# Token scatters of six tiles held back behind VectorE's products of the shared units

## The chip, the cores and the metric

One core of a Trainium2 chip runs the whole kernel. The metric is device time in microseconds of an execution; lower is better. Before the change it is 340.23 us, the median of three runs (339.7 to 340.44).

## The reference

One transformer block with adaptive layer norm on 2 x 1024 tokens of width 256. Attention comes first (causal, one head), then a feed-forward part with a shared expert and 16 routed experts, of which each token uses four.

```python
h = layernorm(x) * (1 + ca) + sa
x = x + ga * attention(h)
h = layernorm(x) * (1 + cb) + sb
probs = softmax(h @ w_router); top_w, top_i = top_k(probs, 4); top_w /= sum(top_w)
routed = sum over the four experts e of top_w[e] * (silu(h @ we1[e]) * (h @ we3[e])) @ we2[e]
shared = (silu(h @ ws1) * (h @ ws3)) @ ws2
x = x + gb * (shared / 5 + routed * 4 / 5)
```

## The kernel before

**Tiles and stages.** The 2048 tokens are 16 tiles of 128, `t` = 0 to 15; tile t is the (t+1)-th, so the eleventh is t = 10. A loop over steps s runs attention with a tile in each of several stages, and sends normed rows to the router. Four tiles make a group. For each group VectorE picks four experts a token (`route_choose`, `route_count`), TensorE counts ranks (`rank`), and VectorE turns them into slots, places in a DRAM tensor `xg_rows` sorted by expert (`route_slots`, which ends in the write of `slot_u`, line 1347, and adds one to `s_slots`).

**Scatters.** GpSimd's `send` writes the rows of a tile to their slots: four indirect DMAs a tile, one for each choice k, 128 rows of 1152 bytes each (line 776). The first 32 are sent inside the loop over steps (`SENDS`). The last 32, tiles t = 8 to 15, go in one call behind the loop. Ahead of a tile's first scatter GpSimd waits for the tile's row and for the slots of its group. Every scatter adds 16 to `s_sent`. Behind the scatters GpSimd's queue holds only the scatters of the routed results (line 817).

**The shared expert.** It is cut into 16 units, `n` = 0 to 15, four (quarters of the hidden width) for each block of 512 tokens. For each unit TensorE computes both products (`gate_up`, lines 1816 to 1818), ScalarE applies silu (`silu_step`, line 911), VectorE multiplies (`g_step`, line 1461; it adds one to `s_g`), and TensorE applies the down product (`down`, line 1990). Units 0 to 11 stand ahead of the routed experts, 12 to 15 behind them. In VectorE's queue the products of units 4 to 11 have between them: the tables of the routed tiles (`route_places`, `route_tables`, `route_marks`), the sums of finished blocks (`shared_out`), and the low parts of the routed weights (`split_routed`, lines 1450 to 1454, 16 subtractions of 128x768, from a table `splits` by n).

**The routed experts.** The sorted rows are cut into 40 pairs of tiles of 128 rows. SyncE loads them from `xg_rows` (`load_rows`, line 645), two loads of 144 KB a pair, into a ring of four pairs. It begins when all 64 scatters have landed. From the fifth pair on a load waits for VectorE's `s_rxlo` of four pairs before. VectorE first copies two words a row (`keep_ends`, line 1744), TensorE transposes the rows (`rows_back`, line 2191), ScalarE and VectorE split them in two parts, TensorE multiplies with the expert's weights, ScalarE applies silu (line 1083), and so on up to GpSimd's scatter of the results.

**The places where it meets.** SyncE's queue around the first load:

```python
if n == 0:
    sp.wait_ge(s_sent, 16 * TILES * TOPK)
if n >= RING:
    sp.wait_ge(s_rxlo, n - RING + 1)
load_rows(n, place[2 * (n % 8):2 * (n % 8) + 2], s_xs[n % RING])
```

TensorE's queue goes `down(11)` for the first two token tiles, `rows_back(0)`, `down(11)` for the other two, `rows_back(1)`, and then the pairs. VectorE's goes `g_step(11)`, `split_routed(15)`, `x_lo_rows(0)` (which begins with `keep_ends(0)`), `shared_out(2)`, and then the pairs.

Of the kernel before, what the change touches and what calls it, by code (L numbers as in the profile page):

```python
# [190 lines left out]
ROUTER_CONSTANTS = 10 + len(TOKEN_RUNS)  # L191


SENDS = {9: 4, 10: 4, 11: 4, 12: 4, 13: 4, 14: 4, 15: 4, 16: 4}


# [39 lines left out]
def adaln_block(nc, x, qkv, o_proj, gamma, beta, w_router, we1, we3, we2, ws1, ws3, ws2, c_in, wmod, out):  # L236
# [3 lines left out]
    with ctx:  # L240
        def sem(name):
            return ctx.enter_context(nc.semaphore(name))
# [253 lines left out]
        def done(eng, stage_, t):  # L496

            if t >= 0:
                eng.wait_ge(tl[stage_], t + 1)
# [11 lines left out]
        s_ab, s_y, s_silu, s_g, s_gated, s_shared = (sem(n) for n in (  # L511
            "gate_up_mm", "down_mm", "silu", "g", "shared_gated", "shared_added"))
# [175 lines left out]
        def _(pool):  # L688
# [33 lines left out]
            def token_numbers():  # L722

                for t, token, count in TOKEN_RUNS:
                    nc.gpsimd.iota(tok_at[:, t:t + count], pattern=[[1, count]], base=token, channel_multiplier=BT,
                                   allow_small_or_imprecise_dtypes=True).then_inc(s_ones2, 1)
# [39 lines left out]
            def send(count):  # L766


                for n in range(sent[0], sent[0] + count):
                    t, k = divmod(n, TOPK)  # L770
                    if n == 0:
                        pool.wait_ge(s_regions, 16 * 5)
                    if k == 0:
                        done(pool, "h2row", t)
                        pool.wait_ge(s_slots, t // BT + 1)
                    nc.gpsimd.indirect_dma_start(  # L776
                        out=xg, out_offset=bass.IndirectOffsetOnAxis(ap=slot_u[:, t, k:k + 1].bitcast(U32), axis=0),
                        in_=hrow[:, t, :], in_offset=None).then_inc(s_sent, 16)
                sent[0] += count

            for s in range(FIRST, LAST + 2):
                if -3 < s < 0:
                    residual(s + 3)
                for m, group in enumerate(norms_of(s)):
                    if s == -3 and m == 1:
                        residual(0)
                    inverse_std(group)
                    for n, t in reversed(group):
                        if n > 1:
                            mean_shift(n, t)  # L790
                if 0 <= s and s + 3 < RESIDUAL_BY_VECTOR:

                    done(pool, "rinv", s - 1)
                    residual(s + 3)
                if s == 3:
                    router_constants()
                if s == 5:
                    token_numbers()
                send(SENDS.get(s, 0))

# [4 lines left out]
            for r in range(RING):  # L805
                nc.gpsimd.memset(sent_all[:, :, r:r + 1], 16.0 * loads_of(NPAIR - RING + r)).then_inc(s_mark_const, 1)
            send(TILES * TOPK - sent[0])


# [1484 lines left out]
```

## Time and profile before

| what | value |
|---|---|
| time, median of 3 runs | 340.23 us (339.7 to 340.44) |
| the profiled execution | span 380.7 us; the page gives no other time for it |
| TensorE busy | 333.3 us (88% of the span), mean granted clock 0.990 |
| VectorE busy | 255.2 us (67%) |
| ScalarE busy | 190.3 us (50%) |
| GpSimd busy | 200.8 us (53%), of it 65.6 in 64 scatters of line 776 and 70.5 in 72 of line 817 |
| DMA | 57.55 MB, mean 151 GB/s |

The span runs from the first to the last instruction of the one execution that the hardware profiler recorded. It is longer than the timed runs, which are taken without the profiler. A share of 0.50 in the granted clock is 1.2 GHz, 1.00 is 2.4 GHz.

### The profile page before, as it was taken

What the parts mean: (1) busy time and instruction counts of PE and PEld (TensorE: products, weight loads), DVE (VectorE), ACT (ScalarE), POOL (GpSimd) and SP (SyncE); (2) the same over time, 40 slices, a digit from 0 to 9 for tenths busy, and PEclk for the clock granted to TensorE, in tenths of its full rate; (3) what the DMA queues carried; (4) which work ended last, traced back from release to release, by engine and by line L of the source; (5) the groups of instructions that cost most, each with busy time, mean ns of one, the idle gap of its engine ahead of it and who ended that gap; (6) DMA issues with size and microseconds to landing.
All of it is one profiled execution on the core that took longest, in us unless ns stands there. A gap on an engine that the chain in (4) does not pass through costs nothing.

```text
span 380.7 us, 7758 instructions
## 1 busy us (share of the span) xinstructions
PE 333.3 (88%) x2252; PEld 297.6 (78%) x2252; DVE 255.2 (67%) x806; ACT 190.3 (50%) x440; POOL 200.8 (53%) x285
## 2 busy tenths in 40 slices
PE   8989999999999999868889897788778877887995
PEld 5778898888899898736778796777667767877784
DVE  1889998999887756219986744543454345448797
ACT  2667777767865665414234444443444355346300
POOL 2687754357867655746740064555455545545820
PEclk9999999999999999969999999999999999999999
DMA  8236600002213996322232466556445544788824
GB/s 271 75 104 205 209 17 27 16 31 87 85 65 118 316 312 214 119 85 78 104 117 76 121 209 183 155 171 194 149 124 171 164 133 136 264 302 327 261 86 165
DMA packets 42280, 57.55 MB, mean 151 GB/s; under 512 B 5144, under 2 KB 34592, under 8 KB 42240
## 3 DMA queue, kind: packets, MB, share of 16 engines
q1 hardware_dynamic: 34288, 35.42, 30.7%
q0 software_dynamic: 6864, 19.80, 13.5%
q10 hardware_dynamic: 1088, 1.84, 1.5%
q8 instruction: 20, 0.33, 0.4%
q14 instruction: 20, 0.16, 0.2%
HBM read 32.64 MB, written 24.40 MB: 150 GB/s over the span
## 4 chain that ended last, share of the span: by engine, by line
PE 43%; DVE 27%; issue 13%; another core or an unknown queue 7%; ACT 7%; DMA 1%; POOL 1%; DVEq 0%; ACTq 0%
PE ps L1816 10%; PE ps L1818 10%; PE ps L1817 9%; PE ps L1990 4%; DVE y_in L1497 3%; DVE r_g L1771 2%; DVE gT_lo L1759 2%; ACT r_silu L1083 2%; DVE negmax L1626 2%; PE ps L2191 2%; PE ps L2092 1%; PE ps L1823 1%; DMA wmod_sb<-in_L_wmod_dram 1%; DVE bn L1197 1%
## 5 line engine op out<-in xcount | busy, mean ns | idle before, releaser
L817 POOL DMA_INDIRECT y_rows<-y_sb,aside x72 | 70.5, 980 | 87.9 <-ACT y_sb L1092 71.7
L776 POOL DMA_INDIRECT xg_rows<-hrow,slot_u x64 | 65.6, 1024 | 27.8 <-issue 20.0
L1816 PE MATMUL ps<-rpool 128*128 128x256 f32 (+3 forms) x152 | 49.8, 328 | 2.7 <-DVE rpool L1221 1.1
L1768 DVE TENSOR_TENSOR aside<-ends,aside 128x2 int32<-128x2 int32 (+1 forms) x40 | 6.3, 157 | 62.9 <-ACT r_silu L1083 55.4
L1816 PE MATMUL ps<-w_hi_routed,xT_hi 128*128 x158 | 45.2, 286 | 1.8 <-DVE xT_lo L1752 1.8
L1083 ACT ACTIVATE r_silu<-ps 128x256 f32<-128x256 f32 x40 | 15.8, 395 | 61.4 <-PE ps L1818 51.4
L1818 PE MATMUL ps<-rpool 128*128 128x256 f32 (+3 forms) x152 | 46.0, 302 | 0.0
L1817 PE MATMUL ps<-rpool 128*128 128x256 f32 (+3 forms) x152 | 45.9, 302 | 0.0
L1818 PE MATMUL ps<-w_hi_routed,xT_lo 128*128 x158 | 44.7, 283 | 0.0
L1817 PE MATMUL ps<-w_lo_routed,xT_hi 128*128 x158 | 44.6, 283 | 0.0
L1816 PE MATMUL ps<-w_hi_routed,gT_hi 128*128 x79 | 25.8, 326 | 15.1 <-DVE gT_lo L1759 15.0
L1816 PEld LDWEIGHTS ps<-rpool 128*128 128x128 f32 x152 | 28.8, 190 | 6.0 <-DVE rpool L1221 2.5
L1816 PEld LDWEIGHTS ps<-w_hi_routed,xT_hi 128*128 128x128 f32 x158 | 30.2, 191 | 2.5 <-issue 2.3
L1752 DVE TENSOR_TENSOR xT_lo<-ps,xT_hi 128x512 fp32r<-128x512 f32 x40 | 27.4, 684 | 6.2 <-ACT xT_hi L1071 6.0
L1817 PEld LDWEIGHTS ps<-w_lo_routed,xT_hi 128*128 128x128 f32 x158 | 30.2, 191 | 0.0
L1818 PEld LDWEIGHTS ps<-w_hi_routed,xT_lo 128*128 128x128 f32 x158 | 30.2, 191 | 0.0
L1816 PEld LDWEIGHTS ps<-w_hi_routed,gT_hi 128*128 128x128 f32 x79 | 14.9, 188 | 19.5 <-issue 19.4
L1818 PEld LDWEIGHTS ps<-rpool 128*128 128x128 f32 x152 | 28.8, 189 | 1.1
L1817 PEld LDWEIGHTS ps<-rpool 128*128 128x128 f32 x152 | 28.9, 190 | 0.9
L1816 PE MATMUL ps<-h2T_hi,w_hi_shared 128*128 128x512 f32 x64 | 27.3, 426 | 1.4 <-issue 0.9
L1071 ACT ACTIVATE xT_hi<-ps 128x512 fp32r<-128x512 f32 x40 | 24.4, 612 | 8.0 <-remote 5.8
L1817 PE MATMUL ps<-h2T_lo,w_hi_shared 128*128 128x512 f32 x64 | 25.6, 400 | 2.6 <-issue 2.6
(236 smaller groups left out, 928.8 us busy)
## 6 DMA issues: line engine op xcount, KB each, us to landing
xs<-xg_rows SPq DMA_DIRECT2D x68, 144.0 KB
y_in<-y_rows SPq DMA_DIRECT2D x16, 512.0 KB
xg_rows<-empty SPq DMA_DIRECT2D x4, 576.0 KB, 3.8
x_in<-in_L_attn_x_dram SPq DMA_DIRECT2D x16, 128.0 KB, 2.1
w_raw_routed<-in_L_ffn_we_dram SPq DMA_DIRECT2D x8, 256.0 KB
out_dram<-x SPq DMA_DIRECT2D x14, 128.0 KB, 1.8
xs_own<-xg_rows SPq DMA_DIRECT2D x11, 144.0 KB
wmod_sb<-in_L_wmod_dram ACTq DMA_DIRECT2D x3, 512.0 KB, 6.6
```

The source lines that it names most:

```text
L776: nc.gpsimd.indirect_dma_start(out=xg, out_offset=bass.IndirectOffsetOnAxis(ap=slot_u[:, t, k:k + 1].bitcast(U32), axis=0), in_=hrow[:, t, ...
L817: nc.gpsimd.indirect_dma_start(out=yb, out_offset=bass.IndirectOffsetOnAxis(ap=dest[:, 2 * n + i:2 * n + i + 1].bitcast(U32), axis=0), in_ ...
L1071: nc.scalar.activation(xT_hi[:, n % 2].rearrange("p i c t -> p (i c t)"), ps[:, 6 + n % 2, :], ACT.Copy).then_inc(s_rxhi, 1)
L1083: nc.scalar.activation(r_silu[:, n % 2], ps[:, n % 2, :].rearrange("p (i w) -> p i w", i=2)[:, :, 0:H], ACT.Silu).then_inc(s_rsilu, 1)
L1497: then(nc.vector.tensor_tensor(y[0], y[0], y[k], ALU.add))
L1626: nc.vector.tensor_reduce(negmax[:, t % 4:t % 4 + 1], score_banks(t), AX.X, ALU.max, negate=True).then_inc(tl["negmax"], 1)
L1752: nc.vector.tensor_tensor(xT_lo[:, n % 2].rearrange("p i c t -> p (i c t)"), ps[:, 6 + n % 2, :], xT_hi[:, n % 2].rearrange("p i c t -> p ...
L1759: nc.vector.tensor_tensor(gT_lo[:, n % 2].rearrange("p i t -> p (i t)"), ps[:, 2 + n % 2, 0:2 * P], gT_hi[:, n % 2].rearrange("p i t -> p ...
L1816: nc.tensor.matmul(dst, w[0], x_[0], start=first, stop=False)
L1817: nc.tensor.matmul(dst, w[0], x_[1], start=False, stop=False)
L1818: return nc.tensor.matmul(dst, w[1], x_[0], start=False, stop=last)
L1990: last = nc.tensor.matmul(to, unit(n)[1][:, tok], w_raw_s[:, e, W2:WX], start=(e == 0 and b < NB - 1 and j % 2 == 0), stop=(e == SH - 1), ...
```

## The change

GpSimd's `send` gets one more wait ahead of the first scatter of tiles t = 10 to 15. Tile 10 waits until `s_g` has reached 5, that is until `g_step(4)`, the fifth product, is done; tile 11 for the sixth, and so on up to tile 15 for the tenth. Tiles 8 and 9 are not held. No instruction is moved on any engine's queue; only these six waits are added.

```diff
+SENT_BEHIND = {10: 4, 11: 5, 12: 6, 13: 7, 14: 8, 15: 9}
 SENDS = {9: 4, 10: 4, 11: 4, 12: 4, 13: 4, 14: 4, 15: 4, 16: 4}
...
                     if k == 0:
                         done(pool, "h2row", t)
                         pool.wait_ge(s_slots, t // BT + 1)
+                        if t in SENT_BEHIND:
+                            pool.wait_ge(s_g, SENT_BEHIND[t] + 1)
                     nc.gpsimd.indirect_dma_start(
```

## Rows read from the trace of the kernel before

**Rows 1.** The page: its head, and the chain by engine.
```profile
span 380.7 us, 7758 instructions
...
PE 43%; DVE 27%; issue 13%; another core or an unknown queue 7%; ACT 7%; DMA 1%; POOL 1%; DVEq 0%; ACTq 0%
```

**Rows 2.** SyncE's queue: its waits (us, times, longest), and its timeline (start, us).
```profile
SPq L644 <- DMA xg_rows<-hrow,slot_u: 9.8, 1, 9.8
...
196.94 0.90 SPq L645 DMA_DIRECT2D xs<-xg_rows  x2
```

**Rows 3.** Timelines of TensorE and VectorE at the first routed rows: start, us, what.
```profile
203.17 4.49 PE L1990 MATMUL ps<-w_raw_shared,act_g 128*128 128x256 f32 x20
207.50 0.60 PE L2191 MATMUL ps<-ident,xs 128*128 128x128 f32 x4
...
208.80 0.60 PE L2191 MATMUL ps<-ident,xs 128*128 128x128 f32 x4
...
207.39 0.23 DVE L1744 TENSOR_SCALAR ends<-xs 128x2 int32 x2
```

**Rows 4.** DMA issues (KB each, us to landing); a window: busy, clock, DMA share, GB/s.
```profile
xg_rows<-empty SPq DMA_DIRECT2D x1, 144.0 KB, 2.1
...
204.50:206.90 2.40, 2.40 (x13) 2.02 (x12) 1.14 (x3) 1.33 (x2) 0.00 (x0) 1.00 0.00 0
```

**Rows 5.** Timeline of GpSimd from the ninth tile's scatters on.
```profile
147.30 1.08 POOL L776 DMA_INDIRECT xg_rows<-hrow,slot_u  x1 [1.12 <-DVE slot_u L1347]
...
166.43 0.96 POOL L776 DMA_INDIRECT xg_rows<-hrow,slot_u  x1 [0.30 <-issue]
173.05 0.96 POOL L776 DMA_INDIRECT xg_rows<-hrow,slot_u  x1 [5.66 <-DVE slot_u L1347]
...
189.85 1.63 POOL L776 DMA_INDIRECT xg_rows<-hrow,slot_u  x1 [0.30 <-issue]
...
194.32 0.96 POOL L776 DMA_INDIRECT xg_rows<-hrow,slot_u  x1 [0.30 <-issue]
219.43 0.96 POOL L817 DMA_INDIRECT y_rows<-y_sb,aside  x1 [24.16 <-ACT y_sb L1092]
```

**Rows 6.** Timeline of VectorE: the last slots, and products 5, 6, 7, 8, 10.
```profile
171.84 0.42 DVE L1347 TENSOR_REDUCE slot_u<-matched 128x16 int32<-128x256 f32 x1
...
172.51 0.68 DVE L1461 SCALAR_TENSOR_TENSOR act_g<-act_g,ps 128x512 f32<-128x512 f32 x1
...
175.72 0.68 DVE L1461 SCALAR_TENSOR_TENSOR act_g<-act_g,ps 128x512 f32<-128x512 f32 x1
...
184.37 0.68 DVE L1461 SCALAR_TENSOR_TENSOR act_g<-act_g,ps 128x512 f32<-128x512 f32 x1
...
188.23 0.68 DVE L1461 SCALAR_TENSOR_TENSOR act_g<-act_g,ps 128x512 f32<-128x512 f32 x1
...
197.20 0.68 DVE L1461 SCALAR_TENSOR_TENSOR act_g<-act_g,ps 128x512 f32<-128x512 f32 x1
```

**Rows 7.** Around 158 to 170: chain; VectorE; windows (PE, PEld, DVE, ACT, POOL, clock, DMA).
```profile
158.68 11.34 another core or an unknown queue
...
170.05 0.22 DVE L1315 TENSOR_TENSOR above<-ps,region 128x64 f32<-128x64 f32 x1 [11.37 <-remote]
...
159.00:162.00 3.00, 1.54 (x6) 0.96 (x6) 0.00 (x0) 1.57 (x3) 2.39 (x3) 1.00 0.41 153
...
165.00:168.00 3.00, 1.85 (x3) 0.68 (x3) 0.00 (x0) 0.00 (x0) 1.93 (x2) 0.50 0.28 108
```

**Rows 8.** Timeline of ScalarE in the routed stage: silu of pairs.
```profile
220.00 0.39 ACT L1083 ACTIVATE r_silu<-ps 128x256 f32<-128x256 f32 x1 [0.84 <-PE ps L1818]
...
222.81 0.39 ACT L1083 ACTIVATE r_silu<-ps 128x256 f32<-128x256 f32 x1
...
236.52 0.38 ACT L1083 ACTIVATE r_silu<-ps 128x256 f32<-128x256 f32 x1 [3.69 <-PE ps L1818]
...
244.14 0.38 ACT L1083 ACTIVATE r_silu<-ps 128x256 f32<-128x256 f32 x1 [3.66 <-remote]
```

## The prediction, made before the changed kernel had run

> **What bounds the kernel now.** I read the page first. The profiled execution spans 380.7 us [rows 1], and the median of the three timed runs is 340.23 us, so 40.5 us of the profile are not in the timed runs. The page gives no other time for that execution. A term read from it may be carried over only if it is a difference between two paths of the same stage, and I choose such differences below. The chain of waits is TensorE's for 43% and VectorE's for 27%. The chain names no scatter and no load of routed rows, so the scatters are off the critical path today.
>
> Second, I asked when the routed rows must be there. SyncE waits 9.8 us for the last scatter (its row names that as the releaser) and issues its first load of sorted rows at 196.94 [rows 2]. TensorE works without a pause through the shared units until 207.50, when it transposes the first routed rows. VectorE reads them first at 207.39 [rows 3].
>
> How long do the rows take from there? The first two loads belong to pair 0, and their two issues take 0.90 us [rows 2]. A load of the same 144 KB with no neighbour took 2.1 us to land [rows 4]. So pair 0 lands 2.1 to 3.0 us after SyncE's start; I estimate 2.7, that is 199.6, for the second issue begins within those 0.90. The far bound is the end of all eight first loads: nothing moves after 204.5 [rows 4]. So today pair 0 waits in SBUF for about 207.4 - 199.6 = 7.8 us. That slack is what the change spends.
>
> Third, GpSimd. Tiles 9 to 12 (eleventh tile is t = 10, so these are t = 8 to 11) go out in one train from 147.30 to 166.43, a scatter each 1.27 us. Then it waits for the slots of the last group, ready at 172.26, and t = 12 to 15 go from 173.05 to 194.32 [rows 5]: 15 steps in 21.27 us. SyncE starts 196.94 - 194.32 = 2.6 us after the last one begins.
>
> **The change, part by part.** It adds six waits on GpSimd's queue, moves no instruction and removes nothing. The product that t waits for is the 5th to the 10th: the 5th starts at 172.51, the 6th at 175.72, the 7th at 184.37, the 8th at 188.23 and the 10th at 197.20, each takes 0.68 [rows 6].
>
> t = 10 and 11. Today they are the second half of the train that ends at 166.43, in an interval in which GpSimd is otherwise free until 173.05. With the change they leave after 173.2 and 176.4: eight scatters more stand ahead of t = 12. A scatter starts 0.8 us after what released it (slots end 172.26, scatter 173.05 [rows 5, 6]), so t = 10 starts at 174.0, t = 11 at 174.0 + 4 x 1.27 = 179.1, done by 184.2.
>
> t = 12. It waits for the seventh product, which ends at 184.37 + 0.68 = 185.05, so it starts at 185.85. Today it is 173.05. The shift is 12.8 us.
>
> t = 13, 14, 15. A tile takes 21.27 / 15 x 4 = 5.7 us, so they are reached at 191.5, 197.2 and 202.9. The products end at 188.9, before 197.2 (the 9th lies ahead of the 10th) and at 197.9: these three waits are met on arrival and cost nothing. What covers them is GpSimd's own pace; were a scatter free, t = 15 would go at 198.7.
>
> The end of the train is 185.85 + 21.27 = 207.1. SyncE starts 2.6 us later, 209.7, and pair 0 is in at 209.7 + 2.7 = 212.4. TensorE and VectorE want it at 207.4. **The new wait is 5.0 us.** Bounds: with no scatter lengthened the train is 15 x 1.27 = 19.05 us and the wait 2.8; if pair 0 took as long as all eight loads do today (204.5), 4.9 us more, but that is four pairs, and the lone load is nearer, so I keep 2.7. What makes the train 2.2 us longer than its shortest are a few scatters of up to 1.63 instead of 0.96 [rows 5] that lie beside VectorE's subtractions of routed weights (lines 1450 to 1454). Ten such subtractions lay in that train, and eleven follow the seventh product, so I keep 21.27.
>
> The Trainium skill has a rule here that speaks against the change ("SBUF — State Buffer", section "Who interferes with whom"): a VectorE instruction with two SBUF inputs and a GpSimd instruction that reads SBUF exclude each other for the whole instruction. By it each of eleven subtractions could hold the train for its full length, some 10 us in all instead of the 2.2 that the train shows over its shortest. The trace agrees with the direction and not with that size.
>
> Does this difference hold in the timed runs? The seventh product to the first routed transposition is 207.50 - 185.05 = 22.4 us of nearly unbroken TensorE work, and the seventh product to landed rows is 0.8 + 21.3 + 2.6 + 2.7 = 27.4. Both start from the same event, so whatever the profile adds before 185 cancels. This is why I measure from the product and not from the clock of the trace.
>
> Who is behind the waits? On GpSimd only the later scatters, then the scatters of results, first at 219.43 [rows 5]; they wait for ScalarE's rows and move with them. SyncE's queue holds the loads. VectorE stands at its first copy from the rows, with its last shared sum behind it, and TensorE at its transposition, with half a unit of the shared down product behind it. So nobody fills the gap. Pair 1 is issued right behind pair 0 and TensorE wants it 1.3 us later (207.50 to 208.80 [rows 3]); what little it may add stays in the range. From there each stage waits for the one before it, and the whole rest moves by 5.0.
>
> **TensorE's clock.** In the span it falls once before the end. It was 1.00, then TensorE was busy 1.54 of 3 us from 159 on, and from 165 to 168 it was 0.50 of 2.4 GHz, that is 1.2 GHz [rows 7]. A gap of 5.0 us is idler than that, so it may fall again. At the lower level the first transpositions and the half unit, 208.80 - 207.50 = 1.3 us of work ahead of everything, take twice as long: +1.3, or 0. I take half, 0.7.
>
> Sum: 340.2 + 5.0 + 0.7 = 345.9.
>
> **The rivals.** *Faster: the burst was the trouble.* From 158.68 the chain holds 11.34 us that the profile puts down to nothing on this core, VectorE waits 11.37 for TensorE's ranks, and TensorE is busy for half of the time from 159 to 162 [rows 7]. This is just when t = 10 and 11 go out, and it ends when their packets are out. If the scatters cause it and the timed runs have it too, the change gives back up to 11.35 and pays 5.0: 340.2 - 6.3 = 333.9. It decides from 5.0 us of stall on. Against it: GpSimd scatters as densely from 173.05 to 194.32 [rows 5] without such a gap, and the DMA share was only 0.41 and 0.28 in the stall [rows 7]. And the routed stage has waits of the same kind, ScalarE idle 3.66 us in every second pair [rows 8]: two pairs take 244.14 - 236.52 = 7.62 us there, where two of the first pairs took 2 x (222.81 - 220.00) = 5.62. Of 40 pairs some 33 go at the slow pace: 16.5 x 2.0 = 33 us, and with the stall 44, near the 40.5 that the timed runs lack. So I read both as the cost of being profiled. The skill has a path for this ("NOTIFIC — the notification-queue block", section "Overflow: three behaviours, one of which stalls the engine"): the records' internal pipeline holds up an engine rather than lose one. No row here shows that pipeline. Chance 0.13.
>
> *No change: the slack is larger in the timed runs.* Without the stall TensorE reaches the routed rows 11.35 earlier and t = 12 goes right behind t = 11, at 167.7 instead of 173.05, 5.35 earlier; slack 7.8 - 11.35 + 5.35 = 1.8, shift 185.85 - 11.35 - 167.7 = 6.8, and again 5.0. Only a shorter train (2.8 at the least by the rows) and a slower TensorE together bring it under 0.7. 340.2. Chance 0.09.
>
> *Slower still:* the timed runs have no slack at all and the clock falls: 6.8 + 1.3 = 8.1, 348.3. It needs TensorE to be 1.8 us faster to the routed rows than in the profile. Chance 0.08.
>
> **How the numbers follow.** The forecast, a starved start of the routed stage, has 0.70; its own range is 2.8 to 5.0 + 1.3 + 1.5 for a longer train, 343.0 to 348.0. Faster has 0.13, no change 0.09, slower still 0.08. "No change" means within 0.2%, 0.7 us, about what a measurement of this kernel can tell. Slower by more is 0.70 + 0.08 = 0.78. The range must leave out at most 2 in 10: it takes in the forecast's own, no change, and nearly all of slower still, 339.8 to 348.4; the faster case stays out.
>
> **What would show it.** In the new profile t = 12 starts 0.8 us after the seventh product, and t = 13 to 15 go without a pause. The last scatter starts some 22 us after the seventh product. SyncE's first load of sorted rows is issued about 2.6 us after that. The first routed transposition has an idle time of 4 to 6 us ahead of it with a load of rows as releaser, and the granted clock shows whether 0.50 comes behind it. The forecast is wrong if TensorE goes from the shared units to the routed rows without a pause. The rival is right if the time falls and nothing like the 11.34 us stands between the rank product and the slots; should only the profiled span get shorter, that stall was the profile's own.

## The result, and the profile after

The changed kernel takes 348.0 us (median of 4 runs, 346.69 to 349.17), the kernel before, on the same chip, 340.34 us (4 runs, 339.7 to 340.47). The ratio is 1.0232, with a 95% interval of 1.021 to 1.0254: 7.7 us slower. The forecast was 345.9, with the range 339.8 to 348.4.

First the page of the changed kernel: head, busy times, clock, and the chain by engine. Its execution took 346.69 us, with a span of 345.0, so unlike that of [rows 1] it is of a piece with the timed runs.

```profile
span 345.0 us, 7758 instructions
...
PE 324.1 (94%) x2252; PEld 297.8 (86%) x2252; DVE 256.0 (74%) x806; ACT 195.9 (57%) x440; POOL 202.3 (59%) x285
...
PEclk9999999999999999999999969999999999999999
...
PE 54%; DVE 21%; issue 10%; POOL 7%; ACT 4%; DMA 2%; DVEq 0%; SPq 0%; ACTq 0%; POOLq 0%
```

GpSimd and the DMA now stand in the chain of what ended last, with 7% and 2%, where they had 1% each [rows 1], and 2% and 1% in the second profile of the kernel before that is shown below. One slice of the clock reads 6, just past the middle. The waits of the same kernel (total us, times, longest):

```profile
SPq L645 <- DMA xg_rows<-hrow,slot_u: 23.3, 1, 23.3
...
POOL xg_rows L779 <- DVE act_g L1464: 7.7, 2, 5.3
...
DVE ends L1747 <- DMA xs<-xg_rows: 6.6, 1, 6.6
PE ps L2194 <- DMA xs<-xg_rows: 6.3, 1, 6.3
```

Two things are new. GpSimd stood twice for a product of VectorE, and TensorE and VectorE each stood once for routed rows that had not landed. The timelines say where. VectorE's seventh product, then GpSimd: the last scatter that goes unheld, the first of t = 10, the first of t = 12, one of the long ones, and the last of all.

```profile
173.46 0.68 DVE L1464 SCALAR_TENSOR_TENSOR act_g<-act_g,ps 128x512 f32<-128x512 f32 x1
...
155.56 0.96 POOL L779 DMA_INDIRECT xg_rows<-hrow,slot_u  x1 [0.30 <-issue]
161.81 0.95 POOL L779 DMA_INDIRECT xg_rows<-hrow,slot_u  x1 [5.28 <-DVE act_g L1464]
...
174.94 0.96 POOL L779 DMA_INDIRECT xg_rows<-hrow,slot_u  x1 [2.38 <-DVE act_g L1464]
...
178.95 1.63 POOL L779 DMA_INDIRECT xg_rows<-hrow,slot_u  x1 [0.30 <-issue]
...
196.63 0.96 POOL L779 DMA_INDIRECT xg_rows<-hrow,slot_u  x1 [0.30 <-issue]
```

SyncE's first load, and TensorE at the seam between the shared and the routed expert:

```profile
199.27 10.77 SPq L646 DMA_DIRECT2D xs<-xg_rows  x12
...
191.19 4.49 PE L1993 MATMUL ps<-w_raw_shared,act_g 128*128 128x256 f32 x20
202.01 1.11 PE L2194 MATMUL ps<-ident,xs 128*128 128x128 f32 x4 [6.33 <-DMA xs<-xg_rows]
...
209.14 0.38 PE L1819 MATMUL ps<-w_hi_routed,xT_hi 128*128 x1 [1.57 <-DVE xT_lo L1755]
```

And windows over the seam (stretch and length, busy time of PE, PEld, DVE, ACT and POOL, granted clock, DMA share, GB/s):

```profile
195.70:198.70 3.00, 0.00 (x0) 0.00 (x0) 0.00 (x0) 0.00 (x0) 1.59 (x2) 1.00 0.29 112
198.90:202.00 3.10, 0.00 (x0) 0.00 (x0) 0.00 (x0) 0.00 (x0) 0.00 (x0) 0.50 0.48 130
202.00:205.50 3.50, 3.49 (x13) 3.03 (x14) 1.64 (x5) 0.60 (x1) 0.00 (x0) 0.50 0.77 224
206.00:209.00 3.00, 1.57 (x14) 1.33 (x12) 2.79 (x10) 1.36 (x3) 0.00 (x0) 1.00 0.25 77
```

Read them together. The seventh product ends at 174.14, and 0.80 later t = 12 starts. The last scatter starts 21.69 us after that, SyncE's first load 2.64 after it, and TensorE has its rows 2.74 after that, at 202.01. TensorE had been done with its shared work since 195.68, and did nothing for 6.33 us. During that pause its clock went to 0.50 (1.2 GHz), and the four transpositions take 1.11 instead of 0.60 us [rows 3]. From the first transposition to the first product of pair 1 it is 209.14 - 202.01 = 7.13 us.

### The profile page after: what moved, and what is told of

Same layout as the page of the kernel before. It is cut to its first block, busy times and chain, and to the rows that moved or that the text cites. A ratio compares the mean times of both kernels' runs of the same rounds, so it can differ in the third digit from the quotient of the medians.

```text
span 345.0 us, 7758 instructions
## 1 busy us (share of the span) xinstructions
PE 324.1 (94%) x2252; PEld 297.8 (86%) x2252; DVE 256.0 (74%) x806; ACT 195.9 (57%) x440; POOL 202.3 (59%) x285
## 4 chain that ended last, share of the span: by engine, by line
PE 54%; DVE 21%; issue 10%; POOL 7%; ACT 4%; DMA 2%; DVEq 0%; SPq 0%; ACTq 0%; POOLq 0%
PE ps L1819 13%; PE ps L1820 12%; PE ps L1821 12%; PE ps L2194 5%; POOL xg_rows L779 5%; DVE y_in L1500 3%; PE ps L1993 3%; PE ps L2220 2%; DVE negmax L1629 2%; PE ps L2095 1%; PE ps L1826 1%; DMA wmod_sb<-in_L_wmod_dram 1%; PE ps L1928 1%; DVE bn L1200 1%; DVE y_in L1510 1%
## 5 line engine op out<-in xcount | busy, mean ns | idle before, releaser
L779 POOL DMA_INDIRECT xg_rows<-hrow,slot_u x64 | 66.6, 1040 | 29.5 <-issue 19.4
L2194 PE MATMUL ps<-ident,xs 128*128 128x128 f32 x136 | 21.3, 281 | 6.3 <-DMA xs<-xg_rows 6.3
L1821 PE MATMUL ps<-h2T_hi,w_lo_shared 128*128 128x512 f32 x64 | 25.1, 392 | 0.0
```

The source lines that it names most:

```text
L779: nc.gpsimd.indirect_dma_start(out=xg, out_offset=bass.IndirectOffsetOnAxis(ap=slot_u[:, t, k:k + 1].bitcast(U32), axis=0), in_=hrow[:, t, ...
L1821: return nc.tensor.matmul(dst, w[1], x_[0], start=False, stop=last)
L2194: last = nc.tensor.transpose(ps[:, 6 + n % 2, (i * DC + c) * P:(i * DC + c + 1) * P], rows_of(n)[i][:, c * P:(c + 1) * P], ident[:])
```

## The experiments

### The kernel before once more

The 380.7 us of [rows 1] fit no timed run. I needed a profile of the kernel before that does. The edit is none.

> The kernel before, unchanged, once more for a second profile. If the 11.34 us stall and the slow pace of the routed pairs (7.62 us for two) were only in that one recorded execution, this profile spans about 338.5 us, as the changed kernel's spans 345.0 at a time of 346.69: no wait of VectorE over 5 us between the rank product and the slots, and pairs 2.81 us apart. TensorE then reaches the first routed transposition at about 195.5 with the load of rows landed 1 to 2 us before. If scatters in a burst stall TensorE in the timed runs too, the stall of about 11 us is there again and the span stays near 338 only because something else is shorter. Time: 340.3, ratio 1.000.

Measured: 339.91 us against 339.95, ratio 0.9997 (0.9972 to 1.0021). The profiled execution took 340.43 us, its span is 338.7. Its windows at the place of [rows 7] (columns as above), its last scatter and first load, and TensorE at the seam:

```profile
span 338.7 us, 7758 instructions
...
159.00:162.00 3.00, 3.00 (x15) 2.54 (x14) 2.86 (x13) 1.22 (x2) 2.19 (x3) 1.00 0.26 100
165.00:168.00 3.00, 3.00 (x15) 2.48 (x14) 2.06 (x4) 2.07 (x3) 2.39 (x3) 1.00 0.34 134
...
190.56 0.96 POOL L776 DMA_INDIRECT xg_rows<-hrow,slot_u  x1 [0.30 <-issue]
...
193.41 9.96 SPq L645 DMA_DIRECT2D xs<-xg_rows  x12
...
196.60 0.60 PE L2191 MATMUL ps<-ident,xs 128*128 128x128 f32 x4
...
202.48 0.38 PE L1816 MATMUL ps<-w_hi_routed,xT_hi 128*128 x1 [1.66 <-DVE xT_lo L1752]
```

TensorE is busy 3.00 of 3 us where it had 1.54 and 1.85, at full clock, and the 11.34 us of stall are not there, although t = 10 and 11 go out at the very same place. So the scatters do not cause it, and the rival "the burst was the trouble" has nothing to give back. The pairs of the routed stage follow 2.81 us apart nearly throughout, so the slow pace of [rows 8] was of that one recorded execution too. What caused it there is not shown.

The same profile gives the true slack. With 2.74 us from first load to use, pair 0 would be usable at 193.41 + 2.74 = 196.15, and TensorE wants it at 196.60. The slack is about 0.45 us, not the 7.8 of the recorded execution. And 202.48 - 196.60 = 5.88 us there become 7.13 after the change: with nearly the same second gap (1.66 and 1.57), the low clock costs 1.25 us. So 6.33 + 1.25 = 7.6 of the measured 7.7 us. The whole way from the end of the seventh product to that first product of pair 1 gives the same: 202.48 - 175.24 = 27.24 us before, 209.14 - 174.14 = 35.00 after, 7.76 more. The spans of the two profiled executions differ by less, 6.3 us, mainly because the one of the changed kernel ended its seventh product 1.10 us earlier; it is also the fastest of its four.

### One tile's wait at a time

The edit is the table alone. For t = 12:

```diff
-SENT_BEHIND = {10: 4, 11: 5, 12: 6, 13: 7, 14: 8, 15: 9}
+SENT_BEHIND = {12: 6}
```

> Only the thirteenth tile (t = 12) waits, for the seventh product. My theory: this one wait sets the start of the last four tiles, so all of the loss is here: last scatter some 21.7 us after t = 12's first, t = 12 at 174.9, gap of TensorE 6.3 us, time 348, +7.7 within 0.7. Rival (each of the six waits, or the spreading of scatters over a longer stretch, costs a part): clearly less, +2 to +5.

Then `{10: 4, 11: 5}` alone:

> Only t = 10 and 11 wait, for the fifth and sixth product. My theory: t = 10 starts at 161.8 as in the changed kernel, t = 11 at 167.3, and t = 12 follows without a pause at about 172.9, 2.1 us earlier than with all six waits: gap of TensorE 6.3 - 2.1 = 4.2 us; time +4.2 if the granted clock stays at 1.00, +5.4 if it falls to 0.50 behind the gap. Rival (the seventh product's wait is all that counts): 0.

Then `{13: 7}`, `{14: 8}` and `{15: 9}`, each alone:

> Only the wait of t = 13 (for the 8th product) is left. Theory: the 8th product ends at 179.10, t = 13 starts at 179.9 instead of about 174.0, the shift is 5.9, less 0.8: gap 5.1 us, and the clock falls as in e3, 1.2 more: 340.0 + 6.3 = 346.3. If the clock stays, 345.1. Rival (only t = 12's wait can cost, the later ones nothing): 340.0.

> Only the wait of t = 14 (for the 9th product) is left. Theory: the 9th product ends at 182.31 in e1's profile, t = 14 starts 0.8 later at 183.1 instead of about 180.0, the shift is 3.1, less 0.8 of slack: gap 2.3 us, clock as before, 342.3. Rival (costs nothing alone either): 340.0.

> Only the wait of t = 15 (for the 10th product) is left. Theory (the slack behind the last scatter is only about 0.8 us in timed executions, as the profiled run of e1 shows against after's; so every hold counts by how far it moves the last scatter, less 0.8): in e1's profile the 10th product ends at 186.97 and t = 15 is reached at about 185.0 + 0.8, so its first scatter moves by about 2.0 us, TensorE's gap ahead of the first routed rows is about 1.2 us, the clock stays at 1.00, and the time is 340.0 + 1.2 = 341.2. Rival (the prediction's 'the waits of t = 13 to 15 are met on arrival and cost nothing'): no change, 340.0, no gap.

TensorE's row at the first routed transposition in each of the five, in the order t = 12; 10 and 11; 13; 14; 15:

```profile
202.54 1.12 PE L2194 MATMUL ps<-ident,xs 128*128 128x128 f32 x4 [6.52 <-DMA xs<-xg_rows]
...
201.86 1.12 PE L2194 MATMUL ps<-ident,xs 128*128 128x128 f32 x4 [5.06 <-DMA xs<-xg_rows]
...
201.12 1.11 PE L2194 MATMUL ps<-ident,xs 128*128 128x128 f32 x4 [5.06 <-DMA xs<-xg_rows]
...
199.09 0.65 PE L2194 MATMUL ps<-ident,xs 128*128 128x128 f32 x4 [2.39 <-DMA xs<-xg_rows]
...
195.96 0.66 PE L2194 MATMUL ps<-ident,xs 128*128 128x128 f32 x4 [0.55 <-DMA xs<-xg_rows]
```

Set beside the end of VectorE's seventh product, an event that all of them share, they fall in line. "First load" is SyncE's first load less the end of that product; the shift is this less the 18.17 of the kernel before (193.41 - 175.24). "Seam" is the time from the first routed transposition to the first product of pair 1, 5.88 us in the kernel before.

| holds | first load | shift | TensorE's gap | shift less gap | lowest clock | seam | time, against before |
|---|---|---|---|---|---|---|---|
| all six | 199.27 - 174.14 = 25.13 | 6.96 | 6.33 | 0.63 | 0.50 | 7.13 | 348.0, 340.34 |
| t = 12 | 199.61 - 174.48 = 25.13 | 6.96 | 6.52 | 0.44 | 0.50 | 7.15 | 347.78, 339.95 |
| t = 10, 11 | 199.13 - 175.25 = 23.88 | 5.71 | 5.06 | 0.65 | 0.50 | 8.14 | 346.91, 339.95 |
| t = 13 | 198.37 - 174.54 = 23.83 | 5.66 | 5.06 | 0.60 | 0.50 | 8.16 | 346.16, 340.07 |
| t = 14 | 196.34 - 175.22 = 21.12 | 2.95 | 2.39 | 0.56 | 1.00 | 5.94 | 343.23, 340.07 |
| t = 15 | 193.13 - 173.90 = 19.23 | 1.06 | 0.55 | 0.51 | 1.00 | 5.94 | 340.57, 340.07 |

Every hold opens a gap as long as the shift of the first load, less 0.4 to 0.7 us of slack, and where the clock falls its share comes on top. Which tile is held matters through where the last scatter ends. The ratios of the rows from t = 12 to t = 14 are 1.0243 (1.0205 to 1.0281), 1.0202 (1.0157 to 1.0247), 1.0177 (1.0155 to 1.0199) and 1.01 (1.0073 to 1.0126). For t = 15 it is 1.0 (0.9981 to 1.002): a gap of 0.55 us is too small to be timed, so the row shows it and the runs neither confirm nor refute it.

The clock's share was not the same in all. In the two profiles with a gap of 5.06 us the seam takes 8.14 and 8.16 us, 2.3 more than before the change and not the 1.25 of the changed kernel. The row that ends it for t = 10 and 11:

```profile
210.00 0.38 PE L1819 MATMUL ps<-w_hi_routed,xT_hi 128*128 x1 [1.57 <-DVE xT_lo L1755]
```

The clock fell there only 1.0 and 0.9 us before TensorE began again, in the changed kernel 3.2 before, and the low stretch was 6.8 us long in each. So more work fell on it, and the shorter gap saved only part of its 1.3 us. Both are the slowest of their four executions (348.07 and 347.19 us), so 2.3 need not hold for the other three.

Two expectations of gaps were missed. For t = 10 and 11 it was 4.2 us and came out as 5.06: t = 12 did go 2.0 us earlier than with all six holds, but its train took 22.25 us instead of 21.69, and the load came 2.82 after its last scatter instead of 2.64. With the larger share of the clock the time was +7.0, where +4.2 or +5.4 was expected. For t = 15 the gap was to be 1.2 and was 0.55: t = 15 was held for 2.0 us as expected, but its four scatters, of which fewer now ran beside long instructions of VectorE, took 4.06 us from first to last instead of 4.79.

The holds do not add: together they cost what the one costs that delays the train most, since a scatter held early waits in time that would be waited later anyway. t = 12 alone is as slow as all six. The waits of t = 13 to 15 are free only while t = 12's stands ahead: alone, t = 13's costs 6.1 us and t = 14's 3.2, near the 6.3 and 2.3 that were expected.

The holds of t = 10 and 11 cost nearly as much, which the recorded execution could not show. There GpSimd was idle for 5.66 us, until 173.05 [rows 5], waiting for slots that the stall had delayed. In the undisturbed execution the slots of the last group end at 161.17, well ahead, and GpSimd has no idle time from t = 8 to t = 15. Its train is one piece, so a pause anywhere in it moves the end, by about its length.

### The gap filled

The changed kernel, with 26 more products on TensorE ahead of the first routed transposition. Nobody reads what they write.

```diff
+            for _ in range(26):
+                nc.tensor.matmul(ps[:, 0, :], w_hi_s[:, 0, 0:P], h2T_hi[:, 0, 0, :], start=True, stop=True)
             rows_back(0)
```

> The changed kernel with 26 extra products of 128x512 on TensorE ahead of the first routed transposition, 26 x 0.228 = 5.9 us, written to a bank that the next product overwrites. My theory: the wait for the rows stays at 6.3 us, of which TensorE now works 5.9, so the clock stays at 1.00 and only the clock's share of the loss goes: from 202.0 to the second pair's first product 5.9 us instead of 7.1, time 346.7, that is +6.4. Rival (the clock costs nothing, the whole loss is the wait): +7.7 as with the change alone.

Measured: 346.33 us, ratio 1.0184 (1.0143 to 1.0226). That is 6.4 us over the kernel before beside it, as expected, where the changed kernel was 7.7 over its own. The two intervals overlap, so the time alone does not settle it; the trace does. TensorE's rows:

```profile
196.28 6.27 PE L2239 MATMUL ps<-h2T_hi,w_hi_shared 128*128 128x512 f32 x26
202.92 0.66 PE L2194 MATMUL ps<-ident,xs 128*128 128x128 f32 x4 [0.37 <-DMA xs<-xg_rows]
...
208.85 0.38 PE L1819 MATMUL ps<-w_hi_routed,xT_hi 128*128 x1 [1.65 <-DVE xT_lo L1755]
```

The clock stayed at 1.00 and 208.85 - 202.92 = 5.93 us, against 7.13 with the gap open and 5.88 in the kernel before. So the pause lowers the clock, and that costs 1.2 us here; the rest is the late rows and stays. In the table above the clock fell for gaps of 5.06 us and more and not for 2.39. What lies between was not tried.

### Real work in the gap

The changed kernel, with what stood behind the late rows moved ahead of them.

```diff
+            shared_out(UNITS_FIRST // SH - 1)
             x_lo_rows(0)
-            shared_out(UNITS_FIRST // SH - 1)
...
-            down(UNITS_FIRST - 1, range(0, BT // 2))
+            down(UNITS_FIRST - 1)
             rows_back(0)
-            down(UNITS_FIRST - 1, range(BT // 2, BT))
             rows_back(1)
```

> The changed kernel with the work that stood behind the late rows moved ahead of them: on TensorE all of the shared down product of unit 11 before the first routed transposition, on VectorE the third shared sum (2.5 us) before the first copy from the rows. Theory (the loss is a starved start; what TensorE and VectorE can do meanwhile comes back): TensorE's gap shrinks by the 0.8 us of the last matmuls at full clock, the second gap of 1.6 us (behind VectorE's sum) goes, so 348.0 - 2.4 = 345.6; the gap of about 5.5 us still lowers the clock to 0.50, which is why it isn't better. Rival (the time is set by the landing of the rows and the pace of pairs alone, and the second gap stands whatever is ahead, since ScalarE holds the second pair's rows back behind its silu): 348.0 - 0.8 = 347.2.

Measured: 347.96 us, ratio 1.0223 (1.0195 to 1.025), no gain over the changed kernel. My theory of 345.6 is refuted. TensorE, and ScalarE at its side:

```profile
202.47 1.11 PE L2194 MATMUL ps<-ident,xs 128*128 128x128 f32 x4 [5.46 <-DMA xs<-xg_rows]
203.96 1.11 PE L2194 MATMUL ps<-ident,xs 128*128 128x128 f32 x4 [0.38 <-DMA xs<-xg_rows]
...
210.01 0.58 PE L1819 MATMUL ps<-w_hi_routed,xT_hi 128*128 x1 [1.16 <-DVE xT_lo L1755]
...
208.04 0.39 ACT L1086 ACTIVATE r_silu<-ps 128x256 f32<-128x256 f32 x1 [3.83 <-PE ps L1821]
208.32 1.17 ACT L1074 ACTIVATE xT_hi<-ps 128x512 fp32r<-128x512 f32 x2
```

The first gap shrank by 0.9 us as it should. The second gap shrank only from 1.57 to 1.16 us, since VectorE's sum was not its only cause: ScalarE copies the rows of pair 1 (208.32) only behind the silu of pair 0 (208.04). The part of the rival that names ScalarE holds, and its 347.2 lies within the interval. In this profiled execution (349.49 us) the clock also stayed at 0.50 for twice as long, 13.7 us, until 213.03, which slows the products ahead of that silu too. The mean clock was 0.978 there and 0.989, 0.988 and 0.985 in the other three, against the changed kernel's 0.99 and once 0.987; how often the long stretch comes is not shown. The other three alone, 346.99 to 348.23 us, are above 345.6 as well.

### Versions that could beat both

That second gap of 1.66 us is in the kernel before too. The edit to the kernel before takes the copy of pair 1 ahead on ScalarE and its low part on VectorE:

```diff
             x_hi(0)
+            x_hi(1)
...
-                if n == 0:
-                    x_hi(1)
...
             x_lo_rows(0)
+            x_lo_rows(1)
             shared_out(UNITS_FIRST // SH - 1)
...
-                if n == 0:
-                    x_lo_rows(1)
```

> The kernel before, with the high and low parts of the second routed pair taken ahead: ScalarE's copy of pair 1 right behind that of pair 0 (was behind the silu of pair 0), and VectorE's low part of pair 1 right behind that of pair 0, ahead of the third shared sum. In e1's profile TensorE stands 1.66 us at 202.48 for this low part. Theory (rows landed early leave a start of the stage that only the order of ScalarE's and VectorE's queues holds back): that gap goes, 340.0 - 1.6 = 338.4. Rival (the sum of 2.5 us now stands ahead of the products of pair 0, and the gap only moves to the third pair): 340.0, within 0.5.

Measured: 339.3 us against 339.92, ratio 0.9991 (0.9975 to 1.0007): not told apart from the kernel before, and not the 1.6 us of the theory. Run again beside the next version:

> The kernel of e8 again, beside e10 on the same chip. Theory: 0.6 us under the kernel before (e8: 339.3 against 339.9) and 0.7 over e10. Rival (e8's 0.6 was chance): as the kernel before.

Measured: 339.32 us against 340.09, ratio 0.9969 (0.9952 to 0.9986). That is a small gain, 0.8 us in the medians. The gap of 1.66 us is gone, but 0.26 and 0.39 us came back at pair 2, where TensorE now waits for VectorE, which does its 2.5 us sum just before. Theory and rival of the first run each had a part:

```profile
203.34 0.44 PE L2215 MATMUL ps<-ident,r_g 128*128 128x128 f32 x2 [0.26 <-DVE r_g L1770]
204.16 0.38 PE L1814 MATMUL ps<-w_hi_routed,xT_hi 128*128 x1 [0.39 <-DVE xT_lo L1751]
```

The last version is that kernel once more changed. It moves the addition of that sum behind the low part of pair 2 and leaves only its two products in front:

```diff
                 if n + 2 < NPAIR:
                     x_lo_rows(n + 2)
+                if n == 0:
+                    shared_add(UNITS_FIRST // SH - 1)
```

> e8 with the third shared sum cut in two: VectorE's two products (1.28 us) stand behind the low part of pair 1, its addition (1.22 us) behind the low part of pair 2. In e8's profile the products of pair 0 start 1.25 us after the end of the shared products, and TensorE then stands 0.25 and 0.39 us for VectorE at the third pair. Theory (the start of the routed stage is VectorE's queue; the 1.66 us gap of the kernel before comes back in full once the whole sum no longer stands there): no gap over 0.3 us, 340.0 - 1.4 = 338.6. Rival (e8 had all there was, since later pairs wait for something else): as e8, 339.3.

Measured: 338.54 us against 340.09 (12 and 23 runs), ratio 0.9963 (0.9945 to 0.9981). Of the waits at the start of the routed stage 0.20 and 0.31 us are left (the first, ahead of pair 0's first product, is in the kernel before too):

```profile
196.81 0.38 PE L1821 MATMUL ps<-w_hi_routed,xT_hi 128*128 x1 [0.20 <-DVE xT_lo L1756]
...
203.43 0.38 PE L1821 MATMUL ps<-w_hi_routed,gT_hi 128*128 x1 [0.31 <-DVE gT_lo L1763]
```

It is faster than both kernels, than the one before by 1.3 us by the ratio and 1.55 in the medians, as expected; that is well under 2%. That it also beats the version with the sum in one piece (0.8 us in the medians) is likely, but the two intervals overlap.

## Why the prediction was right, and where its sizes were off

**What bounds the kernel.** "The scatters are off the critical path today" was right, but barely. The slack of 7.8 us was read from an execution with a stall in front of the seam, and the estimate of 1.8 for the timed runs was still too high: about 0.5. The shift that went with it, 6.8, was nearly right: 6.96.

**t = 12, the step that carries the sum.** Right. t = 12 started 0.80 us after the seventh product, as taken, and no later tile waited. Measuring from that product, and not from a point of the trace's clock, is what saved the sum from the 40 us of disturbance. The wait was 6.3 and not 5.0, and both paths of the difference had their part: scatters to landed rows 27.9 us (0.80 + 21.69 + 2.64 + 2.74) where the text had 27.4, and TensorE 195.68 - 174.14 = 21.5 where it had 22.4. The mis-sized term is the second above all: the disturbed execution was 0.9 us slower even between two points that I took for undisturbed ("nearly unbroken"; the text also says "without a pause"). It has a pause there that the kernel before, profiled again, has not. TensorE's row in the execution of [rows 1], then the same work in the second profile:

```profile
198.63 1.96 PE L1990 MATMUL ps<-w_raw_shared,act_g 128*128 128x256 f32 x8 [1.02 <-DVE gated L1473]
...
187.71 1.96 PE L1990 MATMUL ps<-w_raw_shared,act_g 128*128 128x256 f32 x8
```

**t = 13 to 15** "cost nothing": true of the whole change, and only because t = 12's stands ahead of them. The text said that their cover is GpSimd's own pace; it did not say that without t = 12's wait the cover goes.

**t = 10 and 11** were put "in an interval in which GpSimd is otherwise free". That is a step that failed. In the undisturbed profiles no such interval exists. It did not touch the sum, since t = 12's wait is the longer one, but a change that held only these two would have been forecast far too low: they cost 7.0 us.

**The clock.** The text took half of 1.3. It fell, and cost 1.25 us in the changed kernel, so the whole term belonged in the sum: 5.0 + 1.3 would have given 346.5. The price was right and the half of it was a guess. [rows 7] alone did not decide it: the clock fell there after 1.46 idle of 3 us, yet for t = 14 a pause of 2.39 us left it at 1.00.

**Sum.** 6.3 + 1.25 = 7.6, against 5.7 in the text and 7.7 measured. So the wait was put 1.3 us too low and the clock's term some 0.6.

**The rivals.** "The burst was the trouble" is refuted by the kernel before itself, without the stall. "No change" is refuted: the slack was smaller, not larger. "Slower still" gave 348.3; the result, 348.0, is nearer to it than to the forecast, and by part of its mechanism: hardly any slack behind a TensorE that is faster to the routed rows (0.9 us, not 1.8), and the fallen clock. Forecast and rival were one mechanism with two sizes, which is why the range held. That was partly luck: the forecast's own upper end, 348.0, allows 1.5 us for a longer train, and the train was only 0.4 longer (21.69 against 21.27); the room was used up by the slack, for which the sum had none.

**VectorE beside GpSimd.** By the rule of the Trainium skill, "SBUF — State Buffer", section "Who interferes with whom", the text put some 10 us on eleven subtractions. The train measured 21.69 us against the shortest possible 19.05, so 2.6. The size was wrong, but the rows bear the rule out more than the text allowed. Two scatters of the kernel before, profiled again, each behind the addition of VectorE (two inputs in SBUF) in which it began:

```profile
167.83 1.22 DVE L1479 TENSOR_TENSOR x<-x,gated 128x1024 f32<-128x1024 f32 x1
168.76 1.12 POOL L776 DMA_INDIRECT xg_rows<-hrow,slot_u  x1 [0.30 <-issue]
...
188.19 1.23 DVE L1479 TENSOR_TENSOR x<-x,gated 128x1024 f32<-128x1024 f32 x1
188.76 1.49 POOL L776 DMA_INDIRECT xg_rows<-hrow,slot_u  x1 [0.31 <-issue]
```

When the first began, the addition had 0.29 us to go, and the scatter is 0.16 longer than the usual 0.96; the second had 0.66 to go and is 0.53 longer. But for the first of a train (1.08 in each), the other long scatters of t = 8 to 15 in the profiled executions of both kernels follow the same sum, beside subtractions too: longer by what the instruction still had to run, less about 0.13 (the starts of the single subtractions are estimated from their merged rows). So a scatter waits for the rest of the one instruction in which it begins, 0.2 to 0.7 us in the changed kernel's train, and not for all that run beside it; that is why eleven subtractions cost 2.6 us and not 10. It goes one way: a scatter that began first is not longer, and the rows of two or three subtractions are at most 0.06 us longer for it. At one place two starts are too near to be put in order:

```profile
184.49 1.87 DVE L1453 TENSOR_TENSOR w_lo_routed<-w_raw_routed,w_hi_routed 128x768 fp32r<-128x768 f32 x2
...
184.50 0.96 POOL L776 DMA_INDIRECT xg_rows<-hrow,slot_u  x1 [0.30 <-issue]
185.77 1.42 POOL L776 DMA_INDIRECT xg_rows<-hrow,slot_u  x1 [0.31 <-issue]
```

The scatter of 0.96 us starts within 0.01 of the first of two subtractions and is not held; the next begins within the second and is 0.46 longer.

The rule of the Trainium skill, "NOTIFIC — the notification-queue block", section "Overflow: three behaviours, one of which stalls the engine", still has no row for or against it; that the stall was of the recorded execution alone is shown, its cause is not.

## What to carry to other kernels

When the profiled execution is much longer than the timed runs, take its differences between events of one stage, and distrust every idle interval and every slack in it: here 7.8 us of slack and a pause of 5.7 us on GpSimd stand in an execution with a stall that the second profile, as long as the timed runs, does not have. Even a difference within one stage can carry a pause of it, here 0.9 us. A producer whose work runs in one unbroken train has no free place for a wait: what any wait in it costs is the shift of the train's last item, less the slack at the consumer, and here six waits cost what the worst one costs. Where the consumer was TensorE, pauses of 5 us and more also lowered its clock, and that cost 1.2 to 2.3 us on top of them.

## What the runs showed of the hardware

In the changed kernel the clock fell to 0.50 at 198.77, within TensorE's pause, and stayed there for 6.83 us, until 205.59, so that more than half of the low stretch fell on work that had begun again at 202.01. Pauses of 5.06 (twice), 5.46, 6.33 and 6.52 us lowered it, one of 2.39 didn't. With the two of 5.06 it fell only 1.0 and 0.9 us before the work began again, 5.9 us of work ran at 1.2 GHz, and the seam took 8.1 to 8.2 us instead of 7.1. A scatter of GpSimd that began inside an instruction of VectorE with two inputs in SBUF was longer by the rest of that instruction, less about 0.13 us. And one and the same kernel was recorded with spans of 380.7 and 338.7 us, the longer one with waits that the profile puts down to nothing on the core.
